# Moving turned softmax probabilities between partitions by pairs of score tiles, in a cross-attention kernel

## The reference

```python
# x1: (8, 512, 1024), x2: (8, 512, 1024), D = 64
q = einsum('bcn,dc->bnd', x1, Wq) + bq
k = einsum('bcn,dc->bdn', x2, Wk) + bk[:, None]
v = einsum('bcn,dc->bdn', x2, Wv) + bv[:, None]
attn = softmax(einsum('bnd,bdm->bnm', q, k), axis=2)
out  = einsum('bcm,bnm->bcn', v, attn) + x1
```

## Time and profile before

| | |
|---|---|
| median of 3 runs | 635.35 us (635.34 to 635.87) |
| the profiled execution: its time | 635.0 us |
| the profiled execution: span of its instructions | 633.2 us |
| PE busy | 629.5 us, 99% of the span |
| DVE, ACT, POOL busy | 442.9, 328.2 and 143.3 us |
| `move`'s DMAs, L298 | 240 records of 128 KB, 2.3 us from issue to landing |
| `move_part`'s DMAs, L309 | 56 of 32 KB, 1.8 us from issue to landing |

### The profile page before, as it was taken

One profiled execution on the slowest core, in us unless ns is written; L12 is line 12 of the kernel. 1 busy time (PEld: TensorE's weight loads), 2 busy tenths in 40 slices (PEclk: granted clock), 3 DMA queues, 4 the chain that ended last, 5 costly groups with the idle time before them and its releaser, 6 DMA issues.

```text
span 633.2 us, 13435 instructions
## 1 busy us (share of the span) xinstructions
PE 629.5 (99%) x5318; PEld 590.1 (93%) x5318; DVE 442.9 (70%) x511; ACT 328.2 (52%) x430; POOL 143.3 (23%) x115
## 2 busy tenths in 40 slices
PE   9999999999999999999999999999999999999998
PEld 7888899999999999999999999999999999999986
DVE  6995768847778477794777947778568776597351
ACT  6786535735457345474454653555626547265120
POOL 0332200631007400083000830016300353004100
PEclk9999999999999999999999999999999999999999
DMA  8633426963269532776328762287533974345442
GB/s 334 215 133 83 128 84 181 331 143 111 73 176 324 133 126 82 187 285 166 99 83 204 281 159 89 100 227 260 137 93 114 248 243 114 99 132 133 109 145 81
DMA packets 42758, 102.05 MB, mean 161 GB/s; under 512 B 8176, under 2 KB 10224, under 8 KB 42736
## 3 DMA queue, kind: packets, MB, share of 16 engines
q1 hardware_dynamic: 42736, 101.75, 53.4%
HBM read 51.64 MB, written 16.78 MB: 108 GB/s over the span
## 4 chain that ended last, share of the span: by engine, by line
PE 94%; ACT 2%; SPq 2%; DMA 1%; DVE 1%; issue 0%
PE acc_ps L1158 48%; PE acc_ps L1115 23%; PE s_ps L1080 5%; PE s_ps L1228 4%; PE s_ps L1215 3%; PE acc_ps L1178 3%; PE acc_ps L1353 2%; SPq L298 2%; PE acc_ps L1338 1%; PE s_ps L1082 1%; ACT pt_raw L546 1%; PE acc_ps L1190 1%; PE s_ps L1329 1%; DMA pt_raw<-in_front_dram 1%; ACT pt_raw L552 0%; ACT xs_hi L465 0%
## 5 line engine op out<-in xcount | busy, mean ns | idle before, releaser
L1158 PE MATMUL acc_ps<-pt_hi,vt_hi 64*128 64x512 f32 x960 | 201.5, 386 | 0.2 <-DVE pt_lo L727 0.2
L1158 PE MATMUL acc_ps<-pt_lo,vt_hi 64*128 64x512 f32 x960 | 201.3, 386 | 0.0
L1158 PE MATMUL acc_ps<-pt_hi,vt_lo 64*128 64x512 f32 x960 | 201.3, 386 | 0.0
L1158 PEld LDWEIGHTS acc_ps<-pt_hi,vt_hi 64*128 64x128 f32 x960 | 104.3, 184 | 6.5 <-issue 0.8
L1158 PEld LDWEIGHTS acc_ps<-pt_lo,vt_hi 64*128 64x128 f32 x960 | 104.3, 184 | 5.8
L1158 PEld LDWEIGHTS acc_ps<-pt_hi,vt_lo 64*128 64x128 f32 x960 | 104.3, 184 | 5.8
L1115 PE MATMUL acc_ps<-wv_lo,xs_hi 64*128 64x512 f32 x448 | 95.8, 390 | 0.0
L1115 PE MATMUL acc_ps<-wv_hi,xs_hi 64*128 64x512 f32 x448 | 94.9, 386 | 0.0
L433 POOL TENSOR_TENSOR vt_lo<-vt_lo,v_part 128x64 fp32r<-128x64 f32 x56 | 21.0, 380 | 322.1 <-DVE vt_lo L727 322.1
L558 ACT ACTIVATE probs<-s_ps,negmax 128x1024 f32<-128x1024 f32 x56 | 62.5, 1117 | 54.9 <-DVE negmax L814 54.4
L814 DVE TENSOR_REDUCE negmax<-s_ps 128x1 f32<-128x1024 f32 x64 | 76.7, 1210 | 19.7 <-PE s_ps L1082 18.9
(11 more groups left out here) (140 smaller groups left out, 879.2 us busy)
## 6 DMA issues: line engine op xcount, KB each, us to landing
pt_raw<-blocks SPq DMA_DIRECT2D x240, 128.0 KB, 2.3
stage<-in_x_dram SPq DMA_DIRECT2D x32, 512.0 KB, 6.3
o_sb<-in_x_dram SPq DMA_DIRECT2D x64, 256.0 KB, 3.1
out_dram<-o_sb SPq DMA_DIRECT2D x63, 256.0 KB, 2.1
stage<-in_ctx_dram SPq DMA_DIRECT2D x28, 512.0 KB, 9.0
pt_raw<-in_front_dram SPq DMA_DIRECT2D x4, 512.0 KB, 5.7
v_part<-sums SPq DMA_DIRECT2D x56, 32.0 KB, 1.8
stage<-in_front_dram SPq DMA_DIRECT2D x2, 512.0 KB, 7.6
```

The costliest lines, as they stand in the source:

```text
L1158: mm = nc.tensor.matmul(acc_ps[:, OUT_BANK[group], :], v[rows, m, group * P:(group + 1) * P], p[rows, m, :], start=(swap == 0 and m == 0 a ...
```

## The change

The blocks move by pairs of score tiles ("duos"). A half now has two groups of sixteen DMAs of 64 KB (32 partitions by 2 KB) in place of one group of sixteen of 128 KB, each group with its own semaphore. SP issues a group as soon as its two tiles are turned. `blocks` and `pt_raw` get the duo as their outer index, `pt_rows` and `pair` read runs of 64 queries instead of 128, and q's columns are reordered to match (two copies or two subtractions by the tile's place in its duo, not by half).

In SP's list `move(nb, 0, 0)` and `move(nb, 0, 1)` come ahead of `store(b, 1, 2)` and `store(b, 1, 3)`. Since a first group could now start before `turn(b, 7)`, SP itself waits for the pieces of `pt_lo` of half 0 ahead of the first group of half 1. `turn` waits for its own duo's semaphore, and `p_hi` for both.

```diff
-        blocks = sb("blocks", [P, NQ, MT, NT, Q], F32)
-        pt_raw = sb("pt_raw", [P, NQ, MT, P], F32)
+        blocks = sb("blocks", [P, DUOS, NQ, MT, 2, Q], F32)
+        pt_raw = sb("pt_raw", [P, DUOS, NQ, MT, W], F32)
...
-        pt_rows = pt_raw[:].rearrange("p i m r -> p m i r")
+        pt_rows = pt_raw[:].rearrange("p a i m r -> p m (a i) r")
...
-            return pt[:, 2 * j:2 * j + 2, :].rearrange("p m (i r) -> p m i r", r=P)
+            return pt[:, 2 * j:2 * j + 2, :].rearrange("p m (i r) -> p m i r", r=W)
...
-            def move(b, h):
-
-                sp.wait_ge(s_blk, half_of(b, h) * NT + NT)
+            def move(b, h, a):
+
+                if h == 1 and a == 0:
+                    sp.wait_ge(s_plo, b * DVE_PAIRS + PAIRS // 2)
+                    sp.wait_ge(s_plo_odd, b * 2 + 2)
+                sp.wait_ge(s_blk, half_of(b, h) * NT + 2 * a + 2)
                 for step in range(NQ):
                     for i in range(NQ):
                         j = (i + step) % NQ
-                        sp.dma_start(pt_raw[j * Q:(j + 1) * Q, i, :, :],
-                                     blocks[i * Q:(i + 1) * Q, j, :, :, :].rearrange("p m t r -> p m (t r)")
-                                     ).then_inc(s_moved, 16)
+                        sp.dma_start(pt_raw[j * Q:(j + 1) * Q, a, i, :, :],
+                                     blocks[i * Q:(i + 1) * Q, a, j, :, :, :].rearrange("p m t r -> p m (t r)")
+                                     ).then_inc(s_moved[a], 16)
...
-                move(b, 1)
+                for a in range(DUOS):
+                    move(b, 1, a)
...
                 next_residual(nb, 0, 0)
                 next_residual(nb, 0, 1)
+                for a in range(DUOS):
+                    move(nb, 0, a)
                 store(b, 1, 2)
                 store(b, 1, 3)
-                move(nb, 0)
...
             def first_q_high_b():
                 act.wait_ge(s_qsum, 1)
-                copy(tiles(q_st[0:D, :], 1), by_rows(full, 1)).then_inc(s_qhi, 1)
+                copy(duo_tiles(q_st[0:D, :], 0, 1), duo_rows(full, 0, 1))
+                copy(duo_tiles(q_st[0:D, :], 1, 1), duo_rows(full, 1, 1)).then_inc(s_qhi, 1)
...
                 if j == 0:
-                    act.wait_ge(s_moved, half_of(b, h) * MOVED)
+                    for a in range(DUOS):
+                        act.wait_ge(s_moved[a], half_of(b, h) * MOVED)
...
-                if i == 0:
-                    dve.wait_ge(s_moved, half_of(b, h) * MOVED - MOVED)
+                if i % 2 == 0:
+                    dve.wait_ge(s_moved[i // 2], half_of(b, h) * MOVED - MOVED)
```

More of the change, by code:

```diff
@@ L61 @@
 MOVED = NQ * NQ * 16
+DUOS = NT // 2
+W = 2 * Q
 V_BANK0 = (0, 1, 2, 3, 0, 1, 0, 1)
@@ L123, in build @@
         v_part = sb("v_part", [P, 2, MT, Q], F32)
-        pt_rows = pt_raw[:].rearrange("p i m r -> p m i r")
-        raw = pt_raw[:].rearrange("p i m r -> p (i m r)")
+        pt_rows = pt_raw[:].rearrange("p a i m r -> p m (a i) r")
+        raw = pt_raw[:].rearrange("p a i m r -> p (a i m r)")
         heads = raw.rearrange("p (k n) -> p k n", k=KT)
@@ L133, in build @@
         wq_raw = v_sum[:, KT * D:2 * KT * D].rearrange("p (k d) -> p k d", d=D)
-        probs0 = blocks[:].rearrange("p j m t r -> p (j m t r)").rearrange("p (t n) -> p t n", t=NT)
+        probs0 = blocks[:].rearrange("p a j m t r -> p (a j m t r)").rearrange("p (t n) -> p t n", t=NT)
         probs1 = raw.rearrange("p (t n) -> p t n", t=NT)
@@ L153, in build @@
         s_out = [sem(f"s_out_{i}") for i in range(OUTS)]
-        s_moved = sem("s_moved")
+        s_moved = [sem(f"s_moved_{a}") for a in range(DUOS)]
         s_zero = sem("s_zero")
@@ L244, in turned_blocks @@
         def turned_blocks(i):
-            return blocks[:, :, :, i, :].rearrange("p j m r -> p m j r")
+            return blocks[:, i // 2, :, :, i % 2, :].rearrange("p j m r -> p m j r")
         def pair(pt, j):
-            return pt[:, 2 * j:2 * j + 2, :].rearrange("p m (i r) -> p m i r", r=P)
+            return pt[:, 2 * j:2 * j + 2, :].rearrange("p m (i r) -> p m i r", r=W)
         def by_rows(x, h):
@@ L258, in tiles, with duo_rows, duo_tiles @@
             return x[:, h * NH:(h + 1) * NH].rearrange("p (t i r) -> p t i r", i=NQ, t=NT)
+        def duo_rows(x, t, h=None):
+            part = x if h is None else x[:, h * NH:(h + 1) * NH]
+            return part.rearrange("p (a i t r) -> p t a i r", i=NQ, t=2, r=Q)[:, t, :, :, :]
+        def duo_tiles(x, t, h=None):
+            part = x if h is None else x[:, h * NH:(h + 1) * NH]
+            return part.rearrange("p (a t i r) -> p t a i r", i=NQ, t=2, r=Q)[:, t, :, :, :]
         def half_of(b, h):
@@ L516, in first_q_high_b @@
                 act.wait_ge(s_qsum, 1)
-                copy(tiles(q_st[0:D, :], 1), by_rows(full, 1)).then_inc(s_qhi, 1)
+                copy(duo_tiles(q_st[0:D, :], 0, 1), duo_rows(full, 0, 1))
+                copy(duo_tiles(q_st[0:D, :], 1, 1), duo_rows(full, 1, 1)).then_inc(s_qhi, 1)
             def q_high(b):
                 act.wait_ge(s_qsum, b + 1)
-                for h in range(HALVES):
-                    copy(tiles(q_st[0:D, :], h), by_rows(full, h)).then_inc(s_qhi, 1)
+                for t in range(2):
+                    copy(duo_tiles(q_st[0:D, :], t), duo_rows(full, t)).then_inc(s_qhi, 1)
             def q_second(b):
@@ L769, in first_q_low_b @@
                 dve.wait_ge(s_qhi, 1)
-                sub(tiles(q_st[D:2 * D, :], 1), by_rows(full, 1), tiles(q_st[0:D, :], 1)).then_inc(s_qlo, 1)
+                sub(duo_tiles(q_st[D:2 * D, :], 0, 1), duo_rows(full, 0, 1), duo_tiles(q_st[0:D, :], 0, 1))
+                sub(duo_tiles(q_st[D:2 * D, :], 1, 1), duo_rows(full, 1, 1),
+                    duo_tiles(q_st[0:D, :], 1, 1)).then_inc(s_qlo, 1)
             def first_k_low(h):
@@ L777, in q_low @@
             def q_low(b):
-                for h in range(HALVES):
-                    dve.wait_ge(s_qhi, b * 2 + h)
-                    sub(tiles(q_st[D:2 * D, :], h), by_rows(full, h), tiles(q_st[0:D, :], h)).then_inc(s_qlo, 1)
+                for t in range(2):
+                    dve.wait_ge(s_qhi, b * 2 + t)
+                    sub(duo_tiles(q_st[D:2 * D, :], t), duo_rows(full, t), duo_tiles(q_st[0:D, :], t)).then_inc(s_qlo, 1)
             def k_sum(b):
```

## The result

The changed kernel takes 689.68 us (median; 686.81 to 692.42 in six runs) against 635.61 (634.83 to 635.95) before: the ratio is 1.0854, interval 1.0834 to 1.0874. The forecast was 680, the range 664 to 700.

A forecast was written before the change was run, and what follows sets the result against it. PE's unbroken matmuls bound the kernel, so late data stall it: 27.6 + 6.6 + 2.4 + 4.6 + 3.4 (clock) = 44.6 us on a 633.2 us span, giving a forecast of 680 us, range 664 to 700.

The forecast's parts named there:

- What bounds the kernel: Whole kernel: PE runs matmuls unbroken with one 0.2 us wait; later data cost their whole delay beyond slack.
- The cost of an issue: SP's moves: a 64 KB issue takes 0.628 us, like 128 KB, so a half costs 20.1 us instead of 10.05.
- Half 0: Entry to half 0 of batches 1 to 7: the second group's issues end later, seven stalls, 27.6 us together.
- Batch 0: Half 1 of batch 0: moves end 6.9 us later, 6.6 with the landing, all of it a stall.
- Half 1 of batches 1 to 6: Entry to half 1 in these batches: a stall of about 0.3 to 0.4 us each, 2.4 us for six.
- The last batch: Half 1 of the last batch: PE arrives after 21.76 us, data after 26.4, a stall of 4.6 us.
- The clock: PE's matmuls after stalls: 1.7 us for each of the two longest stalls, 3.4 us, nothing for short ones.
- the rival with the clock falling after every stall: PE after all stalls: seven more stalls at 1.7 us, 12 us more, 692 us; chance 0.17.
- the sign of this miss: In the trace: if PE's waits sum as forecast but the span is longer, the clock is what was missed.
- An issue by the bytes: SP's moves: a 64 KB issue takes 0.31 us, so the time stays at 635.4 us; chance 0.07.
- the shorter issue: SP's moves: issues as the fastest rows, 0.54 us with the gap; stalls of 14.6 us, 650 us; chance 0.08.
- The lost head start: Half 0 moves: a store's landing holds residual loads until turn 3 ends, 5.1 us more in seven batches, 716; chance 0.05.

The follow-up runs named there:

- the kernel before with a faster issue: Kernel before the change, with eight of each half's sixteen 128 KB moves issued by ACT instead of SP: 658.11 us, ratio 1.0279.
- the run with the loads held back: Kernel before, ACT issuing eight of sixteen moves per half, SP waiting for half 0's moves to land before next residuals and loads: 638.04 us, ratio 1.0046.

## Why the prediction was right, and where it was off

**What bounds the kernel** held. PE had no wait to win back, and each us by which its data came late is a us of stall, less the slack read from the rows.

**The cost of an issue** held: 0.62 to 0.63 us were forecast from 128 and 32 KB, and 32 issues of 64 KB take 20.16 us, 0.63 each; the median issue is 591 ns, as it was for 128 KB. The page of the Trainium skill that would have had the change free (DMA: Bandwidth & Descriptors, section Anatomy of one DMA, some 50 ns of dispatch, for GpSimd's DMAs) does not describe SP's issues here: they take twelve times that. The landing, 2.0, was estimated at 2.0.

**Half 0** was forecast at 27.6 us and measured at 26.0. Batches 3 to 7 have 3.33, 3.34, 3.35, 3.34 and 3.15 us for 3.46 each. Batch 1 has 4.89 for 4.05, as both groups ran in code that runs once (SP needed 21.88 us); batch 2 has 4.60 for 6.2, because its 32 issues took 20.58 us and not the 21.38 that were carried over, and began 24.7 us ahead of PE's turn (190.71 against 219.98 - 4.60) where 23.8 were reckoned. **Batch 0** has 6.43 for 6.6.

**Half 1 of batches 1 to 6** was forecast at 2.4 us and is 0. The term of 1.0 us for issues beside the loads was wrong: in batch 3 the 32 issues at 304.14 have a median of 591 ns and take 20.19 us in all, where 20.1 + 1.0 were reckoned, and in batches 2 to 6 they take at most 20.61. And PE comes 1.3 to 2.7 us later to half 1 than reckoned (in batch 3 at 330.32, 27.1 behind its start), since its first matmuls of half 0 are slow. Two slips in this sum nearly cancel: 225.4 - 199.71 is 25.7 and not 25.6, and 67.79 to 70.26 is 2.5 and not 2.4. With two groups in half 1 alone, where no stall of half 0 slows PE, the six cost 0.6 us together. **The last batch** has 2.3 for 4.6, for the same reason; 4.2 without the cold start.

**The clock** is the term that was mis-sized: 3.4 us, against 17.3 of longer matmuls. The granted clock accounts for 15.8 of the 17.3: over the 9 us behind the eight long stalls it reads 0.75, 0.82, 0.73, 0.81, 0.84, 0.67, 0.81 and 0.81; what is missing to 1 adds up to 1.76, and 9 x 1.76 is 15.8. I gave 1.7 us to the two longest stalls and nothing to the others. The size of one was about right: 15.8 us in eight cold stretches is 2.0 each. (Its upper bound was half of the 5.5 us before 6.08; PE's first matmul starts at 0.78, so it is half of 5.3.) The number of cold stretches was wrong. The clock fell behind all eight stalls of 3.15 to 6.43 us, and only behind that of 2.3 it read 1.00. The 3 us behind the stall of 3.15 and behind that of 2.3 (columns as above):

```profile
634.20:637.20 3.00, 2.93 (x14) 2.38 (x16) 2.96 (x6) 1.14 (x4) 2.50 (x5) 0.54 0.11 27
660.00:663.00 3.00, 2.79 (x12) 2.36 (x13) 3.00 (x4) 1.65 (x2) 0.00 (x0) 1.00 0.19 71
```

The length of 3.15 us is no bound. In the kernel before with a faster issue the clock fell behind stalls of 2.09, 2.11 and 2.25 us, and read 1.00 behind one of 2.02 us. The 3 us behind the stalls of 2.02 and 2.11 us:

```profile
127.90:130.90 3.00, 2.97 (x26) 2.52 (x28) 3.00 (x4) 3.00 (x5) 2.50 (x6) 1.00 0.23 90
290.00:293.00 3.00, 2.98 (x18) 2.69 (x20) 3.00 (x4) 3.00 (x5) 2.48 (x5) 0.66 0.34 137
```

Between 2.0 and 2.5 us these runs show both outcomes. So the rival with the clock falling after every stall, at 692 and with a chance of 0.17, had the mechanism. The rule of the Trainium skill on which it leaned (TensorE: Matmul & The Clock Gate, section HAM oscillation) agrees in kind with the trace, where the clock fell behind eight of nine stalls. The prediction had named the sign of this miss: PE's waits about as forecast, and the span longer.

Part of the error was hidden, and that was luck: stalls came out 6.5 us under the forecast (34.7 against 41.2), 4.7 of them in half 1. Some 2.5 of these are slack that the cold stretches gave it (half 1 alone has 0.6 and 4.2 us, the changed kernel 0 and 2.3). The sum on the profiled execution was forecast at 44.6 us and is 51.8; the median lies 2.9 us above that execution.

**The rivals.** An issue by the bytes and the shorter issue fell with the 591 ns. The lost head start did not happen in the changed kernel, and was shown at 722 when it was made to happen.

## What to carry to other kernels

Splitting a transfer to start half of it earlier pays only if the head start is longer than the time that the issuing engine needs for the added DMAs; read the issue's duration from two sizes in the trace before assuming that it falls with the bytes. Where the matmul engine has no wait left, price each late arrival as a stall less the slack of that place, and add the matmuls at the lower clock behind every stall of the lengths seen here, not only the longest: about 2 us each here, behind some of the stalls of 2.1 to 2.5 us and behind all of 2.94 us and more. An engine that is set free earlier starts what is next in its list: look at whose transfers that meets.

## What was not expected of the hardware

Issuing from two queues does not halve the time of the 128 KB moves. With one queue sixteen take 10.05 us. In the run with the loads held back, SP and ACT began half 1 of batch 3 together at 287.32 and needed 7.62 us, and their issues lasted 822 and 976 ns (median) instead of 591. Two stretches of it, in which only these moves run (columns as above; DMA share and GB/s at the end):

```profile
290.00:293.00 3.00, 3.00 (x30) 2.75 (x28) 0.49 (x1) 0.00 (x0) 0.00 (x0) 1.00 0.99 239
293.00:296.00 3.00, 3.00 (x30) 2.75 (x28) 0.00 (x0) 0.08 (x1) 0.00 (x0) 1.00 1.02 272
```

The 16 DMA engines are full at 239 to 272 GB/s there, while they carry 415 where the changed kernel's loads run. One queue issuing 128 KB per 0.628 us asks for 208 GB/s, and in the kernel before the engines are busy for 0.89 of the time at 204 GB/s (264 to 267 us, ahead of batch 3). So the moves of the kernel before are not far from a second limit behind the issue, the DMA engines; cutting them in two met only the first.
